# Attention and feed-forward block: output matmuls of a group in two parts, one at the end of each slot

## The reference

```
h = x @ W1 + b1                       # q, k, v of 16 heads, 8 features each
w = softmax(causal(q @ k.T / sqrt(8)))
a = (w @ v) @ Wp + bp
x = layernorm(x + a)
xr, xk = mu * x + (1 - mu) * x_prev   # for mu_r and mu_k; x_prev: the token before
out = sigmoid(xr @ W_r.T) * (square(relu(xk @ W_k.T)) @ W_v.T)
x = layernorm(x + out)
```

## Time and profile before

| | before |
|---|---|
| median of 3 runs | 766.48 us |
| the profiled execution | 766.06 us |
| its span, first to last instruction | 764.3 us |
| TensorE busy, weight loads | 621.4 us (81%), 279.5 us |
| VectorE, ScalarE, GpSimd busy | 557.7 us (73%), 471.6 us (62%), 378.4 us (50%) |
| mean granted TensorE clock | 0.959 |
| chain that ended last | PE 60%, DVE 21%, ACT 8%, issue 5% |
| output matmuls L510 | 2048 passes, 450 ns each, idle before them 5.5 us in all |
| T L451, idle before | 39.9 us, of which 36.1 us for exps |
| exps L592 | 640, 595 ns each |

### The profile page before, as it was taken

The page is one execution under the profiler, slowest core; times in us unless marked ns, Lnnn a source line. Parts: engine busy times, 40 slices in busy tenths (PEclk is TensorE's granted clock), DMA queues, the critical chain, the costliest instruction groups (busy, mean ns, idle before and its releaser), DMA issues.

```text
span 764.3 us, 18024 instructions
## 1 busy us (share of the span) xinstructions
PE 621.4 (81%) x6733; PEld 279.5 (37%) x6733; DVE 557.7 (73%) x1644; ACT 471.6 (62%) x918; POOL 378.4 (50%) x520
## 2 busy tenths in 40 slices
PE   2256987998988989898989898988989898977743
PEld 2013233434343435343434434343435343433232
DVE  3067777778888887879797978788887978782231
ACT  1111676586767676677777686767676766677510
POOL 6110334355655655565556464655655565455533
PEclk9999999999999999999999999999999999999755
DMA  1241213132331323241413141332323231100100
GB/s 47 96 97 49 94 54 104 44 92 66 79 93 58 112 58 115 45 124 34 118 38 118 40 127 45 75 96 58 112 59 113 54 104 29 47 17 16 29 14 14
DMA packets 65500, 53.19 MB, mean 70 GB/s; under 512 B 10882, under 2 KB 61316, under 8 KB 65412
## 3 DMA queue, kind: packets, MB, share of 16 engines
q1 hardware_dynamic: 65412, 52.03, 24.5%
HBM read 34.70 MB, written 17.30 MB: 68 GB/s over the span
## 4 chain that ended last, share of the span: by engine, by line
PE 60%; DVE 21%; ACT 8%; issue 5%; POOL 2%; DMA 2%; SPq 1%; POOLq 0%; DVEq 0%; ACTq 0%
PE ops L510 15%; DVE rowmax L661 12%; PE sps L487 10%; PE tps L451 10%; PE spare L390 8%; ACT probs L592 6%; PE spare L404 5%; PE sps L472 3%; DVE h L714 3%; PE spare L430 2%; PE spare L417 2%; PE spare L420 1%; PE spare L402 1%; DVE y L703 1%; PE spare L427 1%
## 5 line engine op out<-in xcount | busy, mean ns | idle before, releaser
L661 DVE TENSOR_REDUCE rowmax<-sps 128x1 f32<-128x512 f32 (+7 forms) x1024 | 401.3, 448 | 103.0 <-PE sps L487 102.2
L592 ACT ACTIVATE probs<-tps 128x512 f32<-128x512 f32 x640 | 346.4, 595 | 149.9 <-PE tps L451 149.9
L761 POOL TENSOR_SCALAR_AFFINE_SELECT probs<-probs 128x512 f32<-128x512 f32 x256 | 158.0, 635 | 272.6 <-ACT probs L592 272.6
L510 PE MATMUL ops<-probs,vop 128*32 128x384 f32 (+3 forms) x2048 | 175.7, 450 | 5.5 <-POOL probs L761 4.2
L451 PE MATMUL tps<-qop,kop 50*128 50x384 bf16 (+3 forms) x1024 | 127.5, 307 | 39.9 <-ACT probs L592 36.1
L487 PE MATMUL sps<-kop,qop 48*64 48x512 bf16 (+7 forms) x2048 | 130.6, 310 | 11.9 <-DMA kop<-d_parts 11.9
L472 PE MATMUL sps<-qmask,dup 64*128 64x128 bf16 (+1 forms) x640 | 69.7, 215 | 38.2 <-DVE rowmax L661 34.0
L451 PEld LDWEIGHTS tps<-qop,kop 50*128 50x128 bf16 x1024 | 34.3, 94 | 164.2 <-ACT probs L592 111.5
L510 PEld LDWEIGHTS ops<-probs,vop 128*32 128x32 f32 x2048 | 50.5, 109 | 79.9 <-issue 61.2
L487 PEld LDWEIGHTS sps<-kop,qop 48*64 48x64 bf16 x2048 | 43.1, 106 | 54.5 <-issue 19.6
L472 PEld LDWEIGHTS sps<-qmask,dup 64*128 64x128 bf16 x640 | 31.4, 95 | 80.6 <-DVE rowmax L661 74.2
(11 more groups left out here) (70 smaller groups left out, 601.7 us busy)
## 6 DMA issues: line engine op xcount, KB each, us to landing
d_parts<-qk_parts SPq DMA_DIRECT2D x16, 768.0 KB, 3.8
qop<-d_parts SPq DMA_DIRECT2D x192, 32.0 KB
qop<-d_parts SPq DMA_DIRECT2D x64, 96.0 KB
kop<-d_parts SPq DMA_DIRECT2D x192, 32.0 KB
kop<-d_parts SPq DMA_DIRECT2D x64, 96.0 KB
xa<-L_attn_x SPq DMA_DIRECT2D x16, 256.0 KB, 3.0
xres<-L_attn_x SPq DMA_DIRECT2D x16, 256.0 KB, 3.4
out<-result SPq DMA_DIRECT2D x16, 256.0 KB, 2.5
```

The costliest lines, as they stand in the source:

```text
L510: last = nc.tensor.matmul(ops[32 * t:32 * t + 32, BLK * a:SEQ], vop[:, par, a, QUARTET * half + t, hh, :], probs[:, g % 2, i, off:off + w] ...
L592: nc.scalar.activation(probs[:, g % 2, i, :], tps[:, bank(4 * GROUPS * n + 4 * g + i), :], ACT.Exp, scale=SCALE)\
L661: last = nc.vector.reduce_max(rowmax[:, par, QUARTET * half + i, a:a + 1], sps[:, bank(n), off:off + w], axis=AX_X)
L761: last = nc.gpsimd.affine_select(out=v, in_=v, compare_op=ALU.is_ge, fill=0.0, base=0, pattern=[[0, QUARTET], [1, BLK]], channel_multiplie ...
```

## The change

In each group TensorE now issues the output matmuls of the group before in two parts. The first stands at the end of the first slot, the second at the end of the second slot, each behind the slot's use of the spare bank. Where a strip has two matmuls (384 and 128, or 256 and 256), the first part takes the first and the second part the second; where it has one of 512, it is cut into two of 256 columns. So there are 8 instructions a group in every group, where groups 0 and 2 of five had 4. `masked` and the copy of `ops` are waited for before the first part; `pv_done` is raised after the second.

The rest of the diff is another way to write the same program: uses of the spare bank are listed by name, `late` with `LEAD = 0` returns its arguments, `spare_bank` always returns 0, and waits on the spare bank are counted by use and batch (`COUNTS`). The waits that get another value by this: the q and v matmuls name xT, `xbias` waits for the read of project in place of h, project on VectorE no longer waits for h, and SP's load of `xa` waits for the last xT. On GpSimd, in group 7, the split of the maxima `max0` now stands ahead of the inverse deviation of z, where it stood behind.

```diff
-            def pv(b, entries, par, g):
+            def pv(batch, g, part):
+                par = batch % 2
                 half, c = divmod(g, CHUNKS)
-                if c == 0:
-                    wait(pe, o_copied, 2 * entries + half)
+                if c == 0 and part == 0:
+                    wait(pe, o_copied, 2 * batch + half)
                     if half == 0:
-                        wait(pe, spare_read, last_use(b, "v"))
-                wait(pe, masked, GROUPS * entries + g + 1)
+                        is_read(pe, "v", batch)
+                wait(pe, masked, GROUPS * batch + g + 1)
...
-                for k in range(per_pair):
+                for k in range(per_pair) if per_pair == 1 else range(part, part + 1):
                     for t in range(QUARTET):
                         _, hh, j, i = by_pair[per_pair * t + k]
                         _, _, a, off, w = exp_chunk(c, i)[j]
-                        last = nc.tensor.matmul(ops[32 * t:32 * t + 32, BLK * a:SEQ],
+                        first = BLK * a
+                        if per_pair == 1:
+                            w = w // 2
+                            off, first = off + w * part, first + w * part
+                        last = nc.tensor.matmul(ops[32 * t:32 * t + 32, first:first + w],
                                                 vop[:, par, a, QUARTET * half + t, hh, :],
                                                 probs[:, g % 2, i, off:off + w],
-                                                start=c == 0, stop=c == CHUNKS - 1, skip_group_check=True)
-                last.then_inc(pv_done, 1)
+                                                start=c == 0 and part == 0, stop=c == CHUNKS - 1 and part == 1,
+                                                skip_group_check=True)
+                if part == 1:
+                    last.then_inc(pv_done, 1)
...
                         if active("S", b):
-                            s_masks(b, g, i)
-                            s_chunks(b, 1 - par, g, i)
-                        spare_use(b, par, g, i // 2)
-                    if g == 0 and active("D", b):
-                        pv(b, before("D", b), 1 - par, GROUPS - 1)
-                    elif g > 0 and active("T", b):
-                        pv(b, before("T", b), par, g - 1)
+                            s_masks(before("S", b), g, i)
+                            s_chunks(before("S", b), g, i)
+                        for _, use, n in ORDER[b, g, i // 2]:
+                            spare_use(use, n)
+                        if tg == 0 and active("D", tb):
+                            pv(before("D", tb), GROUPS - 1, i // 2)
+                        elif tg > 0 and active("T", tb):
+                            pv(before("T", tb), tg - 1, i // 2)
...
+        def is_read(eng, use, n, taken=None):
+            if 0 <= n < BATCH and spare_bank(use, n) != taken:
+                eng.wait_ge(spare_read[spare_bank(use, n)], COUNTS[use, n] + 1)
...
-                        wait(pool, h_done, n)
+                        is_read(pool, "project", n - 1)
                         nc.gpsimd.tensor_tensor(xbias[:], xres[:],
...
-                    if g == 2 and active("T", b):
-                        split_max(2 * before("T", b) + 1, b, "max1")
+                    for half, use in enumerate(("max0", "max1")):
+                        for _, due, n in ORDER.get(shifted(b, g, -1), []):
+                            if due == use:
+                                split_max(n, half)
...
-                    if g == 7 and active("S", b):
-                        split_max(2 * before("S", b), b, "max0")
```

More of the change, by code:

```diff
@@ L93, in before, with late, spare_bank, spare_order @@
     return min(max(b + OFFSET[stage], 0), BATCH)
[L96 to L113, removed]
+def late(b, g):
+    t = GROUPS * b + g + LEAD
+    return t // GROUPS, t % GROUPS
+def spare_bank(use, n):
+    return 0
+def spare_order():
+    order = {}
+    for b in range(FIRST_STEP, LAST_STEP + 1):
+        for g in range(GROUPS):
+            for place in range(2):
+                due = [(stage, use, frame) for (stage, use), at in SPARE_USES.items()
+                       for frame, fg in [late(b, g) if stage in LATE else (b, g)]
+                       if at == (fg, place) and active(stage, frame)]
+                assert len(due) <= 1, due
+                order[b, g, place] = [(stage, use, before(stage, frame)) for stage, use, frame in due]
+    return order
+ORDER = spare_order()
+def shifted(b, g, by):
+    at = GROUPS * b + g + by
+    return at // GROUPS, at % GROUPS, 0
+def spare_counts():
+    counts, used = {}, {}
+    for uses in ORDER.values():
+        for _, use, n in uses:
+            k = spare_bank(use, n)
+            counts[use, n] = used.get(k, 0)
+            used[k] = counts[use, n] + 1
+    return counts
+COUNTS = spare_counts()
 def exp_chunk(c, i):
@@ L319, in load_max, with step @@
                             .then_inc(max_in[half], 16)
[L321 to L322 removed]
+            def step(b):
+                par, other = b % 2, 1 - b % 2
                 if active("S", b):
@@ L392, in tokens_by_weights, with spare_use @@
                 return last
[L394 to L398, removed]
+            def spare_use(use, n):
+                k, par = spare_bank(use, n), n % 2
+                spare = spares[k]
+                wait(pe, spare_read[k], COUNTS[use, n])
                 if use == "xT":
-                    wait(pe, xa_in, 16 * (before("X", b) + 1))
+                    wait(pe, xa_in, 16 * (n + 1))
                     for t in range(TT):
@@ L545, in _, with spare_use @@
             act.wait_ge(armed, 1)
[L547 to L549 removed]
+            def spare_use(use, n):
+                if use in ("sums0", "sums1", "project", "value"):
                     return
[L551 removed]
+                k, par = spare_bank(use, n), n % 2
+                spare = spares[k]
                 if use in ("max0", "max1"):
[L553 to L555 removed]
+                    wait(act, max_split, 2 * n + int(use[-1]))
+                is_written(act, use, n)
                 if use == "xT":
[L557 removed]
+                    ins = nc.scalar.copy(xT[:, par], spare[:])
                 elif use == "v":
@@ L673, in layer_norm_moments, with spare_use @@
                 last.then_inc(done_moments, 1)
-            def spare_use(b, par, g, place):
-                stage, use = SPARE_USES.get((g, place), (None, None))
-                if stage is None or not active(stage, b):
+            def spare_use(use, n):
+                if use not in ("q", "k", "sums0", "sums1", "project", "value"):
                     return
-                n = before(stage, b)
-                written = spare_before(b, use) + 1
+                k = spare_bank(use, n)
+                spare = spares[k]
                 if use in ("q", "k"):
@@ L744, in _ @@
+                    if active("S", b):
+                        reduce_chunk(before("S", b), g, 2)
+                        reduce_chunk(before("S", b), g, 3)
+                    for _, use, n in ORDER[b, g, 1]:
+                        spare_use(use, n)
+            run_steps(step)
         @block.gpsimd
```

281 lines of the change are left out of this document (143 added, 138 removed), and 15 rows, old and new, of the table SPARE_USES.

## The result

| | before | after |
|---|---|---|
| median | 767.33 us (4 runs, one more than ahead of the prediction) | 816.14 us (4 runs, 813.77 to 820.86) |
| ratio to before | 1 | 1.065, 95% interval 1.059 to 1.070 |
| profiled execution, span | 766.06, 764.3 us | 815.45, 813.7 us |
| a full step | 40.53 us | 43.03 us |
| the last step with exps | 35.3 us | 43.05 us |

The changed kernel is 6.5% slower. The forecast was 800 us, 4.4% slower, in a range of 766 to 814: the direction and most of the mechanism came true, but the time lies 2 us above the range.

What follows compares the result with a forecast made beforehand. TensorE was taken to lead, busy 36.3 of 40.53 us a step. The terms sum to +2.4, taken as +2.1; 14 steps give 29.4, with first and last steps +34: 766 + 34 = 800 us, range 766 to 814.

Steps and rivals of the forecast that it cites:

- TensorE's own work, second drain: Output matmuls of each group: two blocks pay the 0.14 us change of array shape twice, +1.4 us a step.
- waits of T for exps: Where TensorE stood for T: the first part fills 2.0 us of waits, 0.2 come back, -1.8 us a step.
- waits of output matmuls for the mask: First part needs GpSimd's mask half a group sooner: 1.0 us in group 9 to 0, 0.5 twice, +2.0 a step.
- round trips of the spare bank: Only the second part covers the bank's reads: waits of 0.34, 0.34 and 0.79 us, +1.1 us a step in sum.
- VectorE's stretch and other row maxima: Between groups 6 and 8 VectorE sets the time, so the drains added there hide in TensorE's waits: -0.3 us a step.
- waits of output matmuls for the copy of the sums: First part in groups 1 and 6: the prediction has no such wait, 0 us a step.
- The first rival (drain hidden): Output matmuls: weights pulled ahead hide the change of shape, 0.02 us each, +14 us to 780 us; chance 0.13.
- "Elsewhere a matmul of 1.06 to 1.09 stands between, and it waits for nothing.": Groups outside 9 to 0, 3 and 8: a matmul ahead of the first part covers the mask, no wait.
- GpSimd's order: "nothing": Group 7 on GpSimd: split of the maxima ahead of the deviation of z, nothing waits for either, no cost.
- the ring: Last step with exps: T of second slot, mask, first part, T of next second slot; walk 33.0 to 37.0, +3.5 us.
- the clock as a thing not counted: TensorE's clock not granted for longer stretches than now would be a cause not counted; no size given.
- The rival with xbias late: Groups 3 and 4: xres 1.1 us later delays the mask behind xbias, 0.5 us more a step, 809 us; chance 0.12.

Runs made afterwards that it cites:

- the light mask: Changed kernel with GpSimd masking only 8 of the 128 columns of each diagonal block, output no longer correct: 786.1 us, ratio 1.022.
- exchanged parts: Changed kernel with the 128-column part ahead of the 384 one, and the two of 256 in a half's last group exchanged: 803.5 us, ratio 1.047.
- Two runs that take the wait away in different manners: Changed kernel with ScalarE's copy of the sums ahead of the exps, 784.8 us; changed kernel with output matmuls issued in groups 1 and 6 uncut, 780.6 us.
- GpSimd's old order: Changed kernel with the split of the maxima in group 7 back behind the inverse deviation of z: 819.2 us, ratio 1.066.
- the copy first: Changed kernel with ScalarE's copy of the sums ahead of the first exps of groups 1 and 6: 784.8 us, ratio 1.020.
- the first blocks whole: Changed kernel with the output matmuls issued in groups 1 and 6 uncut at the end of the group: 780.6 us, ratio 1.014.
- three buffers and split parts: Changed kernel with exp buffers for three groups in place of two and both parts half a group later: 746.1 us, ratio 0.971.
- the parts together: Changed kernel with both parts at the end of the second slot, one behind the other: 757.4 us, ratio 0.983.
- GpSimd's order alone: Kernel before with one edit, the split of the maxima ahead of the inverse deviation of z in group 7: 758.25 us, ratio 0.988.
- the three edits together: Changed kernel with the copy ahead of the exps, parts exchanged and GpSimd masking 8 of 128 columns, output no longer correct: 744.6 us, ratio 0.969.
- whole blocks and three buffers: Three exp buffers, output matmuls uncut, each block at the next group's second slot or the following group's first, against the kernel before: 716.4 us, ratio 0.934.

## Why the prediction was wrong

By start-to-start times of one step (q matmul to q matmul, 361.35 and 336.61), block cost subtracted:

| term, us a step | predicted | measured |
|---|---|---|
| TensorE's own work, second drain | +1.4 | +1.42 |
| waits of T for exps | -1.8 | -2.1 |
| waits of output matmuls for the mask | +2.0 | +1.84 |
| round trips of the spare bank | +1.1 | +1.1 |
| VectorE's stretch and other row maxima | -0.3 | -1.46 |
| waits of output matmuls for the copy of the sums | 0 | +1.86 |
| sum | +2.4, taken as +2.1 | +2.66 by these terms; +2.50 from step to step |

- *Own work:* right. A part of 256 columns costs 0.57 us, one of 384 and one of 128 together 1.14. The first rival (drain hidden) is out.
- *Exps, mask, bank:* right in size, and in place but for a fourth wait for the mask, 0.27 us in group 7; 0.35, 0.34 and 0.83 us for the three round trips. The run with the light mask (0.94 us a step) and the one with exchanged parts (0.8) show that mask and bank are on the path.
- *"Elsewhere a matmul of 1.06 to 1.09 stands between, and it waits for nothing."* This is the step that failed. It asked only for the mask. In groups 1 and 6 the first part also waits on `o_copied`, a wait that was in the code and that the diff keeps, `if c == 0 and part == 0`. Half a group later the copy has been done in every full step, so the trace of before shows no such wait there. It does show two in the last step with exps, where TensorE comes to the block sooner, and the prediction used that step without them. From its waits (684.29 to 719.60):

```profile
PE ops L510 <- ACT osum L599: 1.3, 2, 0.7
```

  Moved ahead, the part finds the copy still behind two exps on ScalarE. In the first slots of groups 1 and 6 only the short transpose of the row maxima (0.41 us to the next start) stands between S and the part, so nothing covers the wait. Size: +1.86 us a step. Two runs that take the wait away in different manners give most of it back (1.70 us a step and, without the two drains and the round trip that go with it, 1.3); other waits take the rest.
- *VectorE:* mis-sized, -1.46 for -0.3. By the two traces some 0.7 of it is h, 1.11 us for 1.80, no longer beside GpSimd's split and mask; no run takes that part alone. The rest is TensorE coming later to the same row maxima: with the copy wait gone, 0.6 us of their waits is back. The two errors took most of each other away in the step, so 2.5 for 2.1 looks better than it was.
- *GpSimd's order: "nothing".* Wrong for the kernel before, where it is worth 9 us. For the changed one no difference can be told, but not for the reason given: the prediction didn't look at what GpSimd's order does to h.
- *The rest:* a step makes 14 x 0.4 = 6 us of the 15 that are missing. The last step with exps grew by 7.7 us for 3.5: the ring was seen, but not the copy waits in it (1.5 us and, in the second half, 1.7), and its mean granted clock is 0.76 for 0.90 in the earlier trace rows. The other 5 to 6 us have two causes. One is TensorE's clock, at half rate (1.2 for 2.4 GHz) in more stretches. Between 77 us and the last q matmul the kernel before has three short ones, 10 us in all, and steps with one take 42.1 for 40.5 us; the changed kernel has 24 us in all, and a step with two takes 45.8 for 43.0. That is about 3.5 us. The prediction named the clock as a thing not counted, and its range gave it no room.
- *The rival with xbias late came true in a few steps.* That is the other cause. The changed kernel has steps of 44.38, 43.67 and 43.24 us at the full clock. In the longest, from 512.1 us on, xbias waits 2.3 us for xres and the output matmuls 2.9 us for the mask behind it, for 1.6 in the step shown above. From the waits of 512.1 to 556.5:

```profile
PE ops L558 <- POOL probs L814: 2.9, 4, 1.7
POOL xbias L869 <- DMA xres<-L_attn_x: 2.3, 1, 2.3
```

  In all three steps the added wait for the mask is the added time (1.35, 0.64 and 0.2 us), together 2.2 us. In the kernel before, xbias waits 1.9 to 2.2 us in four of the eleven steps from 157 us on, against the 1.19 of the earlier trace rows, and no step pays for it. The one step that was read did not show how late this transfer can be.
- *The range:* its upper end was the rival with xbias late, and no bound stood for the copy wait.

What stays open is why the clock falls. Between 150 and 670 us there are 9 stretches of half clock in the changed kernel with GpSimd's old order, 4 in the changed kernel, with the copy first and with the parts exchanged, 3 in the kernel before and with the light mask, 2 with the first blocks whole, 1 with three buffers and split parts, and none in the runs with the parts together, with GpSimd's order alone, with the three edits together and with whole blocks and three buffers. Each count is from one execution. The kernels that wait least tend to have fewest, but the changed kernel and the one with the old order wait alike and differ most. No run changed the clock's behaviour by itself.

## What to carry to other kernels

When a block is moved ahead, list every semaphore that it and its first instruction wait on, not only the one that it seems to be about, and find for each when it will be raised; a wait that the trace shows at zero has only been covered. Look for that wait in every stage of the trace, the last step too. Read a transfer's lateness over many steps and not in one. Splitting a block to fill a gap paid the change of shape twice here; giving the producers one more buffer and moving the whole block later filled the gaps without a new wait and left 0.5 us of them. And an order on GpSimd that no one waits for can still set how long VectorE takes.

## What the runs showed of the hardware

- The fp32 block of four column strips costs 0.14 us beyond its streaming each time the array goes on to another shape: 1.00 us whole, 0.57 twice in halves, 0.785 + 0.36 for 384 and 128 columns, at the full clock. The Trainium skill's rule (TensorEngine Tiling (Array Packing), Key Properties) that changing the tiling mode drains the array agrees; at which end of the block it is paid no run separates.
- Four VectorE operations of 128x128 f32 with two scalars each take 1.11 us beside GpSimd's power on 128x4 or beside nothing, 1.33 beside its split, 1.43 us partly beside a mask, and 1.80 us beside its split and mask. The loss is in one of the four, which takes up to 1.04 us for 0.34 and ends 0.1 us after GpSimd's work. The Trainium skill (GPSIMD Engine Reference, Specifications) says that GpSimd shares SBUF interfaces with VectorE; the trace agrees that something is shared, which ports is not shown by it.
- With the block together and GpSimd reordered, a step is 0.34 us shorter, 5 us in all. The other 4 to 5 us go with the three stretches of half clock, 1.5 us each, which the kernel before has between 150 and 670 us and this one has not; whether they went because TensorE waits less is not shown.
